# Expert ranks from one comparison and its transposed view, and part of layer 0's ranking on GpSimd

## What is computed

```python
def _L0_cond_ref(x, t_emb, router_W, router_bias, w1, w3, w2, W1e, W2e):
    ...
    s = jax.nn.sigmoid((jnp.concatenate([xf, tf], axis=-1) @ router_W).astype(jnp.float32))
    sel_scores = s + router_bias
    _, topk_idx = jax.lax.top_k(sel_scores, K)          # K = 2 of E = 8
    s_sel = jnp.take_along_axis(s, topk_idx, axis=1)
    denom = s_sel.sum(axis=1, keepdims=True)
    gates = jnp.where(denom > 1e-09, s_sel / (denom + 1e-09), 1.0 / K)
    ...
x = x + _L0_ffn_ref(_L0_cond_ref(x, cond, ...), ...)    # relu^2 experts, top 2 of 8
x = x + _L1_ffn_ref(_L1_cond_ref(cond, x, ...), ...)    # GRU over 128 steps, then top 2 of 8
x = x + _L2_ffn_ref(_L2_cond_ref(x, ...), ...)          # low rank mix, then top 2 of 8
x = x + _L3_ffn_ref(_L3_cond_ref(x, cond, ...), ...)    # RNN over 128 steps, then top 3 of 12
```

## Time and profile before

| | |
|---|---|
| median of 3 runs | 621.6 us (620.53 to 621.81) |
| the profiled execution | 620.77 us, span 619.0 us, mean granted TensorE clock 0.996 |
| TensorE (PE) busy | 599.6 us, 97% of the span |
| VectorE (DVE) busy | 344.8 us, 56% |
| ScalarE (ACT) busy | 287.0 us, 46% |
| GpSimd (POOL) busy | 110.6 us, 18% |
| chain that ended last | PE 84%, DVE 10%, ACT 3%, issue 2% |

### The profile page before, as it was taken

One profiled execution on the slowest core, in us unless ns is written; L12 is line 12 of the kernel. 1 busy time (PEld: TensorE's weight loads), 2 busy tenths in 40 slices (PEclk: granted clock), 3 DMA queues, 4 the chain that ended last, 5 costly groups with the idle time before them and its releaser, 6 DMA issues.

```text
span 619.0 us, 12422 instructions
## 1 busy us (share of the span) xinstructions
PE 599.6 (97%) x4526; PEld 561.2 (91%) x4526; DVE 344.8 (56%) x1221; ACT 287.0 (46%) x955; POOL 110.6 (18%) x328
## 2 busy tenths in 40 slices
PE   8889999999999999999999999999999999999996
PEld 7678888889999999999999999999989889898995
DVE  4874655755455455355553554148947654775514
ACT  3365655646655455445564456646833323311210
POOL 3034111111111111111111110000211321222410
PEclk9999999999999999999999999999999999999999
DMA  8997000000000000000000000090201102002000
GB/s 261 376 287 126 2 1 2 2 2 1 2 2 1 1 2 2 2 2 1 2 1 1 2 2 2 1 199 7 104 2 59 50 5 103 6 5 104 10 1 9
DMA packets 47478, 26.99 MB, mean 44 GB/s; under 512 B 28425, under 2 KB 42681, under 8 KB 46905
## 3 DMA queue, kind: packets, MB, share of 16 engines
q1 hardware_dynamic: 45392, 25.71, 15.5%
q10 hardware_dynamic: 2024, 0.48, 0.4%
HBM read 25.61 MB, written 0.57 MB: 42 GB/s over the span
## 4 chain that ended last, share of the span: by engine, by line
PE 84%; DVE 10%; ACT 3%; issue 2%; POOL 0%; DVEq 0%; POOLq 0%
PE Y L1376 33%; PE U L1376 30%; PE HH L1376 8%; PE ZR L1376 7%; PE M L1376 5%; DVE acc_a L819 2%; ACT gated L653 1%; DVE acc_b L819 1%; DVE rh L819 1%; DVE rank L851 1%; DVE cmp_a L811 1%; DVE fresh L819 0%; ACT cand L631 0%; DVE cmp_b L811 0%; ACT scaled_hi L703 0%
## 5 line engine op out<-in xcount | busy, mean ns | idle before, releaser
L1376 PE MATMUL Y<-l_dn,gated 128*128 128x128 f32 x1152 | 162.7, 284 | 1.8 <-DVE acc_a L819 1.0
L1376 PEld LDWEIGHTS Y<-l_dn,gated 128*128 128x128 f32 x1152 | 141.1, 192 | 3.3 <-issue 2.0
L653 ACT ACTIVATE gated<-U,b1T 128x256 f32<-128x256 f32 x256 | 106.7, 473 | 0.0
L1376 PE MATMUL U<-l_x_hi,l_up_hi 128*128 128x256 f32 x256 | 82.8, 323 | 0.0
L635 ACT ACTIVATE h<-ZR,rnn_b 128x8 f32<-128x8 f32 x128 | 34.2, 267 | 90.0 <-PE ZR L1376 87.6
L819 DVE SCALAR_TENSOR_TENSOR fresh<-zr_s,cand 128x8 f32<-128x8 f32 x128 | 21.4, 167 | 94.4 <-ACT cand L631 92.0
L1376 PE MATMUL U<-l_x_hi,l_up_lo 128*128 128x256 f32 x256 | 72.1, 282 | 0.0
L1376 PE MATMUL U<-l_x_lo,l_up_hi 128*128 128x256 f32 x256 | 72.0, 281 | 0.0
L555 POOL TENSOR_SCALAR zh<-zr_s 128x8 f32<-128x8 f32 x128 | 25.7, 201 | 251.8 <-ACT zr_s L627 251.8
L631 ACT ACTIVATE cand<-HH 128x8 f32<-128x8 f32 x128 | 22.7, 177 | 96.5 <-PE HH L1376 96.5
L1376 PE MATMUL U<-scaled_hi,l_up_hi 128*128 128x256 f32 x192 | 57.7, 301 | 0.0
(11 more groups left out here) (263 smaller groups left out, 1199.0 us busy)
## 6 DMA issues: line engine op xcount, KB each, us to landing
l_bc<-dw SPq DMA_DIRECT2D x4, 1536.0 KB, 7.0
stage<-L_ffn_W_dram SPq DMA_DIRECT2D x4, 768.0 KB, 11.6
w_raw<-L_ffn_W_dram SPq DMA_DIRECT2D x12, 256.0 KB, 6.8
l_up_raw<-L_ffn_W_dram SPq DMA_DIRECT2D x1, 2048.0 KB, 9.8
l_up_raw<-L_ffn_w_dram SPq DMA_DIRECT2D x1, 2048.0 KB, 13.9
l0f_up<-L_ffn_w_dram SPq DMA_DIRECT2D x1, 768.0 KB, 6.8
l0f_dn<-L_ffn_w_dram SPq DMA_DIRECT2D x1, 768.0 KB, 8.7
x<-x_dram SPq DMA_DIRECT2D x1, 512.0 KB, 4.0
```

Of the source, the lines that this page charges most:

```text
L653: last = nc.scalar.activation(gated[:, n % 4, h * N:(h + 1) * N], U[n % 2][:, h * N:(h + 1) * N], ACT.Gelu, bias=b1T[:, col:col + 1])
L1376: return nc.tensor.matmul(out, lhsT, rhs, start=start, stop=stop, skip_group_check=shared)
```

## The change

All rankings: `other >= mine` is made once, multiplied by `earlier` (1 where the other expert has the lower number), and the result's own transposed view is subtracted from it (`both`). The sum of `both` over the others is the rank less (n - 1 - a) for expert a, so the mask compares with `limits`, a row with one value for each expert, in place of a constant. That is three wide operations and the reduction where there were four and the reduction. `earlier8` and `earlier12` become one array `earlier`, of which the 8-expert rankings take a corner. VectorE makes `limits` with four small instructions, behind a wait for `consts`, ahead of its wait for `m_full`.

Layer 0's first tokens: in slot 2 VectorE adds the bias for all 1024 tokens, ranks the first 256 completely in `cmp_a` and `cmp_b`, and makes the comparison for the other 768 (`not_less` into `relu[:, 0]`, 384 elements), which it signals with `ge_made`. GpSimd takes it from there: multiplication, subtraction of the transposed view, and three additions that halve the row (192, 96 and 48 results) in place of a reduction; it signals `ranked_c`. VectorE waits for `ranked_c` in slot 6 and makes the mask; parts 0 and 1 in slots 4 and 5 are gone, parts 3 to 5 stay in slots 7 to 9.

```diff
@@ gpsimd
-            for t, n in ((earlier8, E), (earlier12, E3)):
-                pool.affine_select(out=t[:, :, :], in_=t[:, :, :], compare_op=ALU.is_gt, fill=0.0,
-                                   base=0, pattern=[[1, n], [-1, n]], channel_multiplier=0).then_inc(consts, 1)
+            pool.affine_select(out=earlier[:, :, :], in_=earlier[:, :, :], compare_op=ALU.is_gt, fill=0.0,
+                               base=0, pattern=[[1, E3], [-1, E3]], channel_multiplier=0).then_inc(consts, 1)
+            g = T * B // P - TILES
+            least, both = [relu[:, i, 0:g * E * E].rearrange("p (g a b) -> p g a b", g=g, a=E) for i in range(2)]
+            pool.wait_ge(consts, 4)
+            pool.wait_ge(ge_made, 1)
+            own(nc.gpsimd.tensor_tensor(out=least, in0=least, in1=earlier[:, 0:E, 0:E].unsqueeze(1).to_broadcast([P, g, E, E]),
+                                        op=ALU.mult))
+            own(nc.gpsimd.tensor_tensor(out=both, in0=least, in1=least.rearrange("p g a b -> p g b a"), op=ALU.subtract))
+            own(add(least[:, :, :, 0:4], both[:, :, :, 0:4], both[:, :, :, 4:8]))
+            own(add(both[:, :, :, 0:2], least[:, :, :, 0:2], least[:, :, :, 2:4]))
+            add(rank[:, at(TILES * E, g * E)].rearrange("p (g a) -> p g a", g=g), both[:, :, :, 0], both[:, :, :, 1]).then_inc(ranked_c, 1)
@@ vector, rank_compare and rank_mask_top
-                    own(tt(ca, other, mine, ALU.is_gt))
+                    own(not_less(scores, g, n, room[0]))
-                    own(tt(cb, other, mine, ALU.is_equal))
+                    own(tt(least, least, earlier[:, 0:n, 0:n].unsqueeze(1).to_broadcast([P, g, n, n]), ALU.mult))
-                    own(tt(cb, cb, earlier[:, :, :].unsqueeze(1).to_broadcast([P, g, n, n]), ALU.mult))
+                    own(tt(both, least, least.rearrange("p g a b -> p g b a"), ALU.subtract))
-                    own(tt(ca, ca, cb, ALU.add))
+                    own(v.tensor_reduce(out=grp(rank, g, n), in_=pairs(room[1], g, n), axis=AX.X, op=ALU.add))
-                    own(v.tensor_reduce(out=grp(rank, g, n), in_=ca, axis=AX.X, op=ALU.add))
-                    own(ts(mask[:, 0:g * n], rank[:, 0:g * n], k - 0.5, ALU.is_lt))
+                    own(tt(grp(mask, g, n), grp(rank, g, n), limit.unsqueeze(1).to_broadcast([P, g, n]), ALU.is_lt))
@@ vector, set-up, ahead of dve.wait_ge(m_full, 1)
+            dve.wait_ge(consts, 4)
+            for first, n, chosen in ((0, E, 2), (E, E3, 3)):
+                limit = limits[:, at(first, n)]
+                own(v.tensor_reduce(out=limit, in_=earlier[:, 0:n, 0:n], axis=AX.X, op=ALU.add))
+                own(ts(limit, limit, chosen - 0.5 - (n - 1), ALU.add))
@@ vector, route_c
-                    own(tt(grp(gap_c, g, E), grp(sig_c, g, E), bc[:, 0:E].unsqueeze(1).to_broadcast([P, g, E]), ALU.add))
-                    rank_compare(gap_c, g, E, room, (0,))
-                if 1 in parts:
-                    rank_compare(gap_c, g, E, room, (1, 2))
+                    own(tt(grp(gap, GX, E), grp(sig_a, GX, E), bc[:, 0:E].unsqueeze(1).to_broadcast([P, GX, E]), ALU.add))
+                    rank_compare(gap_c, g, E, (cmp_a, cmp_b))
+                    rank_mask_top(g, E, (cmp_a, cmp_b), r + [top, den_c])
+                    not_less(gap[:, g * E:GX * E], GX - g, E, relu[:, 0, :]).then_inc(ge_made, 1)
                 if 2 in parts:
-                    rank_mask_top(g, E, 2, room, r + [top, den_c])
+                    dve.wait_ge(ranked_c, 1)
+                    rank_mask_top(g, E, None, r + [top, den_c], (1,))
@@ vector, slots
-                            route_c(range(TILES), (0, 1, 2))
+                            route_c(range(TILES), (0,))
-                    if quarter == 3 and REST_C <= n < REST_C + 6:
+                    if quarter == 3 and REST_C + 2 <= n < REST_C + 6:
```

More of the change, by code:

```diff
@@ L195, in adaln_ffn_program @@
         rank_mask = sb("rank_mask", [P, B])
-        earlier8 = sb("earlier8", [P, E, E])
-        earlier12 = sb("earlier12", [P, E3, E3])
+        earlier = sb("earlier", [P, E3, E3])
+        limits = sb("limits", [P, E + E3])
         ones_row = sb("ones_row", [1, N])
@@ L369, in adaln_ffn_program @@
         zeros, scaled_odd = sem("zeros"), sem("scaled_odd")
+        ge_made, ranked_c = sem("ge_made"), sem("ranked_c")
         soft_gap, soft_tanh, comb_ready = sem("soft_gap"), sem("soft_tanh"), sem("comb_ready")
@@ L505, in _ @@
                 own(pool.memset(t[:, :, :], 0.0))
-            own(pool.memset(earlier8[:, :, :], 1.0))
-            own(pool.memset(earlier12[:, :, :], 1.0))
+            own(pool.memset(earlier[:, :, :], 1.0))
             pool.memset(ones_row[:, :], 1.0).then_inc(consts, 1)
@@ L525, in _, with add @@
                                base=R - 1, pattern=[[R, B]], channel_multiplier=-1).then_inc(consts, 1)
-            for t, n in ((earlier8, E), (earlier12, E3)):
-                pool.affine_select(out=t[:, :, :], in_=t[:, :, :], compare_op=ALU.is_gt, fill=0.0,
-                                   base=0, pattern=[[1, n], [-1, n]], channel_multiplier=0).then_inc(consts, 1)
+            pool.affine_select(out=earlier[:, :, :], in_=earlier[:, :, :], compare_op=ALU.is_gt, fill=0.0,
+                               base=0, pattern=[[1, E3], [-1, E3]], channel_multiplier=0).then_inc(consts, 1)
+            def add(out, in0, in1):
+                return nc.gpsimd.tensor_tensor(out=out, in0=in0, in1=in1, op=ALU.add)
+            g = T * B // P - TILES
[8 more added lines that the diff above has]
+            add(rank[:, at(TILES * E, g * E)].rearrange("p (g a) -> p g a", g=g), both[:, :, :, 0], both[:, :, :, 1]).then_inc(ranked_c, 1)
             pool.wait_ge(m_free, m_of("mid", 1) + 1)
@@ L828, in by_tile, with pairs @@
                 return bank[:, 0:TILES * D].rearrange("p (i d) -> p i d", i=TILES)
-            def rank_compare(scores, g, n, room, parts=range(3)):
[L832 to L836, removed]
+            def pairs(t, g, n):
+                return t[:, 0:g * n * n].rearrange("p (g a b) -> p g a b", g=g, a=n)
@@ L837, in rank_compare, with not_less @@
+            def not_less(scores, g, n, least):
+                s = grp(scores, g, n)
+                return tt(pairs(least, g, n), s.unsqueeze(2).to_broadcast([P, g, n, n]),
+                          s.unsqueeze(3).to_broadcast([P, g, n, n]), ALU.is_ge)
+            def rank_compare(scores, g, n, room, parts=range(3)):
+                least, both = [pairs(t, g, n) for t in room]
                 if 0 in parts:
-                    own(tt(ca, other, mine, ALU.is_gt))
+                    own(not_less(scores, g, n, room[0]))
@@ L846, in rank_mask_top @@
+            def rank_mask_top(g, n, room, r=R12, parts=range(2)):
                 score, sig_a, sig_b, rank, mask, gap, top, den = r
-                ca, cb = [t[:, 0:g * n * n].rearrange("p (g a b) -> p g a b", g=g, a=n) for t in room]
+                limit = limits[:, 0:E] if n == E else limits[:, E:]
                 if 0 in parts:
-                    own(tt(ca, ca, cb, ALU.add))
+                    own(v.tensor_reduce(out=grp(rank, g, n), in_=pairs(room[1], g, n), axis=AX.X, op=ALU.add))
@@ L1110, in route_f_quarter @@
                     if place in (3, 4):
-                        rank_mask_top(TILES, E, 2, (cmp_a, cmp_b), parts=(place - 3,))
+                        rank_mask_top(TILES, E, (cmp_a, cmp_b), parts=(place - 3,))
                     if place in (5, 6, 7):
@@ L1169, in routing @@
                         if back == 2:
-                            rank_mask_top(TILES, E, 2, (cmp_a, cmp_b))
+                            rank_mask_top(TILES, E, (cmp_a, cmp_b))
                         if back == 3:
@@ L1411, in router_c @@
                 pe.wait_ge(ld_first, 16 * FIRST)
-                pe.wait_ge(consts, 5)
+                pe.wait_ge(consts, 4)
                 mm(M[0][:, 0:B], cond[:, :], ident[0:B, 0:B])
```

11 lines of the change are left out of this document (1 added, 10 removed).

## The result

The changed kernel took 623.91 us (median of 22 runs, 622.89 to 639.69) against 621.64 (22 runs) for the kernel before on the same chip: a ratio of 1.0038, 95% interval 1.0027 to 1.0049. It is slower by 1.5 to 2.4 us where 2.8 us faster were forecast. The ratios, but not the medians, leave out disturbed executions (TensorE at half clock for some 40 us from about 58 us on; four of e6's twelve, whose median without them is 625.14), in which the profiles of the first comparison, of e5 and of e8 fell; so the rows "after" are those of e1, the same kernel, with a span of 620.7 us, and of those three only times before 52 us are used.

The account below looks back on a forecast made before the run. TensorE sets the pace nearly everywhere, VectorE from 17.0 to 31.2 us. Gains of 1.6 + 0.95 + 0.2 = 2.75 us off the median 621.6 gave 618.8 us, range 617.0 to 620.8.

Parts of the forecast that it names:

- The change moves no DMA. So `c0` moves from 31.72 to 30.75: Ahead of the first F unit: `c0` next waits for ScalarE's copies behind the unmoved `l1_dn` load, gaining 0.95 us.
- one new wait of 1 to 2 us: TensorE ahead of the first F unit: three earlier waits for VectorE close and this wait takes their place.
- the row of 41.18 us: TensorE's wait at 41.18 us for VectorE in the first F ranking: to come at about 39.6, 1.6 us earlier.
- GpSimd's part: Five operations for the 768 tokens, 3.5 us with gaps, 15.8 to 19.3 us; VectorE never waits, 2.9 us to spare.
- the 1.0 that was taken: Up to `c0`: VectorE's small operations held while GpSimd runs, 0 to 2 us in all, taken as 1.0.
- The transposed view: All rankings: subtracting it costs no more than a plain operation, saving 0.32 us a ranking, 1.09 in layer 3.
- The `rh` waits: F rankings of chunks 1 to 3: three TensorE waits of about 0.4 us shrink by 0.32 each, 0.95 us.
- where the sum had 0.2: After the F rankings: 0.1 us for layers 1 and 2 together, 0.1 in front of layer 3.
- TensorE's clock falls in the new wait: Rival: ahead of the first F unit, half clock for 4 us costs about 1.5 us, giving 620.3; chance 0.07.
- GpSimd is the new bound: Rival: GpSimd's five operations exceed 9.6 us and delay `c0`; at 17 us the kernel takes 626; chance 0.05.
- the lock eats the first gain: Rival: GpSimd holds VectorE over 2.2 us, shrinking the 0.95 and 0.3 gains, giving 620.1; chance 0.16.
- The load does not bind: Rival: `l1_dn` lands 2 us earlier, gaining TensorE's 2.25 us before 31.2 and not 0.95, giving 617.0; chance 0.08.

Follow-up runs that it names:

- e6: The kernel before with the changed kernel's SBUF addresses (`earlier8` a corner of `earlier12`, plus a filler): 627.07 us, ratio 1.0050 to the kernel before.
- the first comparison: The changed kernel against the kernel before, 22 runs each: 623.91 us against 621.64, ratio 1.0038.
- e5: The changed kernel with `limits` widened to 64 columns, so later tensors keep their old addresses: 620.0 us, ratio 0.9972 to the kernel before.
- e8: The changed kernel at the old addresses, with the 768 tokens ranked on VectorE and not GpSimd: 620.11 us, ratio 0.9980 to the kernel before.
- e1: The changed kernel run again unaltered, in a second comparison: 622.97 us, ratio 1.0026 to the kernel before.
- e14: The changed kernel with `limits` declared behind the large tensors, which start 256 bytes below their old place: 618.6 us, ratio 0.9963 to the kernel before.
- e12: The changed kernel with 20 unused products on TensorE ahead of its wait for `c0`: 622.73 us, ratio 1.0017 to the kernel before.
- e7: The changed kernel at the old addresses, with ScalarE's first two `up_high` moved behind `mid_copies`: 618.13 us, ratio 0.9943 to the kernel before.
- e3: The changed kernel with ScalarE's first two `up_high` moved behind `mid_copies`: 618.38 us, ratio 0.9949 to the kernel before.
- e9: The changed kernel with `limits` 48 floats wide, later tensors 64 bytes below their old place: 623.74 us, ratio 1.0051 to the kernel before.
- e10: The changed kernel with `limits` 56 floats wide, later tensors 32 bytes below their old place: 623.39 us, ratio 1.0035 to the kernel before.
- e2: The changed kernel with ten unused products on TensorE ahead of its wait for `c0`: 622.42 us, ratio 1.0017 to the kernel before.

## Why the prediction was wrong

**The step that failed** is one sentence: "The change moves no DMA. So `c0` moves from 31.72 to 30.75". It moves none in the program, but it moves where all of them write. The load of `l1_dn` landed 3.67 us later, `c0` came 2.68 us later than before instead of 0.97 earlier, and a hole of 4.28 us stood where "one new wait of 1 to 2 us" was expected. The same belief priced the rival in which the load lands at another time ("nothing in the change touches the queue") and looked only for an earlier one. The last sentence of the prediction names a load that lands at another time among what would make it wrong; it had no price.

**With the addresses repaired the gain comes, somewhat smaller.** e14 is the changed kernel with one line elsewhere: 618.6 us, where 618.8 was forecast, a ratio that makes 2.3 us (the sum said 2.75). e5, the same work at another aligned place, has 620.0 and a ratio that makes 1.7 us. The executions of both spread alike (618.25 to 620.77 for all but one of e5's, 618.36 to 621.8 for e14's) and the intervals overlap, so that e14's median falls within 0.2 us of the forecast is in part luck. Its first F product is 0.59 us earlier than before (0.95 in the sum), the row of 41.18 us stands at 39.80 (39.6 forecast).

In e1's profile the lag behind the kernel before can be followed: 2.69 us at the first F product, 2.56 at the last F down product (0.76 gained in the F phase by the work, 16.04 us before against 15.28 in e12, and 0.63 lost to the clock), 2.17 at the same product of chunk 3 (134.87 against 132.70), 1.67 at the end (622.44 against 620.77).

**GpSimd's part** went as forecast. POOL's timeline in e1:

```profile
16.23 1.00 POOL L537 TENSOR_TENSOR relu<-relu,earlier 128x384 f32<-128x384 f32 x1 [9.25 <-DVE relu L825]
17.30 1.10 POOL L539 TENSOR_TENSOR relu<-relu 128x384 f32<-128x384 f32 x1
18.49 1.01 POOL L531 TENSOR_TENSOR relu<-relu 128x192 f32<-128x192 f32 x2
19.58 0.28 POOL L531 TENSOR_TENSOR rank<-relu 128x48 f32<-128x48 f32 x1
```

3.4 us of work (3.2 forecast), ended at 19.86, and the view costs at most 0.1 us (1.10 against 1.00). VectorE's rows of e1 around it:

```profile
18.24 0.42 DVE L1046 COPY acc_a<-Y 128x256 f32<-128x256 f32 x1 [2.17 <-PE Y L1389]
18.70 0.41 DVE L825 TENSOR_TENSOR comb_x<-sig_a,mask 128x16 f32<-128x16 f32 x1
...
23.56 0.21 DVE L825 TENSOR_TENSOR mask<-rank,limits 128x48 f32<-128x48 f32 x1
...
29.47 0.44 DVE L825 TENSOR_TENSOR den<-den,okay 128x6 f32<-128x6 f32 x1
29.95 0.21 DVE L825 TENSOR_TENSOR comb_x<-comb_x,den 128x48 f32<-128x48 f32 x1
```

There is no wait for `ranked_c`, and the 2.17 us idle ahead of 18.24 confirm that slot 2's additions are hidden. The holding is seen at 18.70 (0.41 where such operations take 0.17) and at 29.47 (0.44, beside GpSimd's work on `pair_w`): 0.5 us, within the 1.0 that was taken. The mask comes at 23.56 and not at 22.2, and VectorE is ready for `c0` at 30.16 and not at 29.5. The bank at 18.24 came 1.1 us later than the 17.14 of the earlier trace rows: TensorE, too, waited 0.31 us for a load at 12.72 and ran at 0.50 from 12.5 to 16 us instead of 0.56. In e7, with the loads at their old speed, VectorE starts `c0` at 29.70: forecast 29.5.

**The transposed view** was taken as free and is not. Groups of DVE instructions by shape in e1 (busy us, mean ns of one, idle before):

```profile
L825 DVE TENSOR_TENSOR cmp_b<-cmp_a 128x128 f32<-128x128 f32 x13 | 5.2, 397 | 0.3
L825 DVE TENSOR_TENSOR cmp_a<-cmp_a,earlier 128x128 f32<-128x128 f32 x13 | 3.8, 292 | 0.4
L825 DVE TENSOR_TENSOR l_cmp_b<-l_cmp_a 128x864 f32<-128x864 f32 x4 | 6.9, 1727 | 0.1
L825 DVE TENSOR_TENSOR l_cmp_a<-l_cmp_a,earlier 128x864 f32<-128x864 f32 x4 | 4.2, 1056 | 0.1
```

The subtraction takes 397 ns where a plain operation takes 292, and 1727 where it takes 1056. A ranking saves 0.21 us and not 0.32, one of layer 3 saves 0.42 and not 1.09. The argument "VectorE's own price does not depend on views" was drawn from broadcasts alone.

**The `rh` waits** close where the forecast said, and yield less. PE's waits from 42 to 134 us (in total, times, longest), before and then in e1:

```profile
PE HH L1376 <- DVE rh L819: 2.7, 9, 0.5
```

```profile
PE HH L1389 <- DVE rh L833: 1.7, 7, 0.3
```

Of the three waits that were named, those at 69.91 (0.42) and 111.96 us (0.46) are gone, and that of 123.50 (0.42) is down to 0.19, at 125.66 in e1; the one just ahead of the second grew from 0.23 to 0.33, and waits for `h_gru` grew from 0.8 to 1.0. The 1.0 us against 0.95 is the waits alone. The lag of e1 shrank only by 0.39 us from the last F down product of chunk 0 to that of chunk 3, and by 0.37 and 0.39 in e3 and e7. Behind it, where the sum had 0.2, another 0.50 were gained (0.4 in e3, 0.55 in e7); no row here tells which ranking gave them. From 134 to 372 us TensorE is busy 235.75 us against 235.59, so it is not less work of its own. The two terms together were 1.15 in the sum and 0.9 in e1.

**The rivals.** "TensorE's clock falls in the new wait" happened in kind (0.50 from 36 to 38 us), but behind a hole of 4.28 us and not of 1 to 2; behind the 1.18 us of e14 the clock stays at 1.00. In e5, which has the forecast's own situation, a new wait of 1.64 us, it fell too; there the F phase took 15.49 us, 0.24 more than in e14. The price of 1.5 us was about right for the first comparison, e9 and e10 (1.6) and too high for e1 (0.63): of the half-clock time a part is time in which TensorE waits for VectorE anyway (1.4 us in e14 between 20 and 42 us for `acc_a`, none in e1). "GpSimd is the new bound" and "the lock eats the first gain" did not happen. Two rivals were mispriced from their own terms: "The load does not bind" adds up to 617.6 against the median, not 617.0 (2.25 + 0.3 + 0.32 + 0.95 + 0.2 off 621.6), and "GpSimd is the new bound" to about 627.5, since its 6 is already 17 less 9.6 less 1.5 and the 1.5 is taken off again. The slower side came from a cause that none of the rivals had.

## What to carry to other kernels

A tensor that is added, dropped or resized moves all that is laid out behind it. Before trusting "no DMA is touched", work out where the destinations of the large loads begin: at a multiple of 256 bytes if it can be had, since no load here was clearly slower for it. Declare small new tensors behind the large ones. And when a load turns out to be the next bound, its landing time is a term of the sum with a range of its own, also on the late side; an order in which nobody on the path waits for it (e3) makes the kernel indifferent to it.

## What the runs showed of the hardware

The place of a destination in SBUF changes the landing time of a load by up to 1.4 times for pieces of 128 bytes (10.8 against 15.6 us for 768 KB, e14 against e1); all packets of that queue together took 14.9 to 15.5% of the engines' time at a multiple of 256, 16.3% at −128 and 18.1 to 19.6% at the other shifts. VectorE pays for a transposed view of an operand that lies in SBUF with 32-bit elements: 1.36 times with 128 elements, 1.64 times with 864; GpSimd pays 1.1 times with 384. Left open: in e2 and e12 the granted clock was 1.00 from 12.5 to 17 us, where all other kernels show 0.50 to 0.70, although the products that were added run after 29 us; no run here tells why. And the profiled executions of e12 and e14 show a further stretch at 0.57 (62 to 66 and 58 to 62 us) that other executions of e14 cannot all have had, since their median of 618.6 us lies 1.7 below its profiled one, 620.32.
